# Moving VectorE's scaling of a finished pair between the two one-hots of the next, and dropping every second pace count on GpSimd

## The reference

```
for _ in range(3):
    x = segment_sum(vals[:, None] * x[cols], rows, num_segments=18750)
    acc = acc + x
out = acc / 4
rating = users_emb[users] @ items_emb.T + bias_user[users] + bias_item.T
return sigmoid(rating)
```

## Time and profile before

| what | us |
|---|---|
| median of 3 runs (lowest, highest) | 5386.34 (5384.41, 5394.33) |
| the profiled execution's own time | 5386.6 |
| its span, from first to last instruction | 5384.8 |
| VectorE busy | 4793.2 (89%) |
| TensorE busy (matmul) | 3361.2 (62%) |
| ScalarE busy | 2443.1 (45%) |
| GpSimd busy | 2415.1 (45%) |
| first halves, first to last scatter | about 1454 to 2288, 2715 to 3546, 3973 to 4807 |

### The profile page before, as it was taken

How to read it: one execution, slowest core, us unless ns; L and a number is a source line. 1 busy time by engine, 2 the same in 40 slices (tenths; PEclk the granted TensorE clock), 3 DMA queues, 4 the chain that set the end, 5 groups by cost and what they waited for, 6 DMA issues and landing times.

```text
span 5384.8 us, 195868 instructions
## 1 busy us (share of the span) xinstructions
PE 3361.2 (62%) x71235; PEld 2864.2 (53%) x71473; DVE 4793.2 (89%) x7569; ACT 2443.1 (45%) x4368; POOL 2415.1 (45%) x2161
## 2 busy tenths in 40 slices
PE   5600021111288888777678888867768888867767
PEld 4500011110277777666567777756657777766652
DVE  9989999999999999877799999967789999977778
ACT  0035555553366666500156666620046666640027
POOL 0038763330177777700067777730037777760000
PEclk9955555555699999999999999989989999989989
DMA  9960000300188778799968878889968777879999
GB/s 329 415 260 0 0 0 3 5 0 0 64 248 253 248 246 247 234 321 328 279 213 251 248 256 249 249 276 328 328 191 255 249 245 246 249 241 328 328 281 357
DMA packets 840272, 1191.20 MB, mean 221 GB/s; under 512 B 150792, under 2 KB 667583, under 8 KB 839825
## 3 DMA queue, kind: packets, MB, share of 16 engines
q1 hardware_dynamic: 716032, 816.66, 53.2%
q0 software_dynamic: 123872, 372.78, 18.0%
q10 hardware_dynamic: 304, 1.00, 0.1%
HBM read 638.35 MB, written 551.90 MB: 221 GB/s over the span
## 4 chain that ended last, share of the span: by engine, by line
DVE 28%; DMA 28%; issue 20%; POOL 9%; PE 6%; ACT 5%; SPq 1%; DVEq 1%; POOLq 0%; another core or an unknown queue 0%; ACTq 0%
DMA ring<-posts 15%; DMA posts<-ring 9%; POOL posts L775 9%; DVE store L1064 6%; PE psum L1501 4%; DVE total L861 3%; ACT new L695 3%; DVE store L1042 3%; DVE ring L1271 3%; DVE store L1043 2%; DMA out<-new 2%; DVE new L1243 2%; DVE ring L1256 2%; DVE ring L1295 2%; DMA ring<-lanes_d 1%
## 5 line engine op out<-in xcount | busy, mean ns | idle before, releaser
L775 POOL DMA_INDIRECT posts<-ring x1884 | 1852.6, 983 | 1740.6 <-DVE ring L1256 1154.0
L1477 PE MATMUL psum<-store,ring 128*128 x45216 | 2086.2, 197 | 497.9 <-DVE ring L1271 461.6
L1477 PEld LDWEIGHTS psum<-store,ring 128*128 128x128 bf16 x45216 | 1815.1, 100 | 769.2 <-issue 591.4
L695 ACT ACTIVATE new<-new 128x512 bf16<-128x512 uint8 x1884 | 1067.8, 614 | 0.0
L1271 DVE TENSOR_SCALAR ring<-ring,lane_f 128x1024 bf16<-128x1024 bf16 x1884 | 959.7, 551 | 23.4 <-DMA ring<-lanes_d 22.0
L1295 DVE TENSOR_TENSOR ring<-ring,wide_lane 128x1024 bf16<-128x1024 bf16 x948 | 612.9, 688 | 300.1 <-ACT ring L705 300.1
L1256 DVE TENSOR_TENSOR ring<-new 128x1024 bf16<-128x1024 bf16 x942 | 652.2, 692 | 93.8 <-ACT new L695 63.3
L693 ACT ACTIVATE ring<-new 128x512 bf16<-128x512 bf16 x942 | 585.9, 622 | 310.3 <-DVE new L1243 308.2
L750 POOL TENSOR_TENSOR ring<-store 128x1024 f32<-128x1024 f32 x157 | 369.6, 2354 | 660.6 <-DVE store L982 306.3
L1243 DVE TENSOR_TENSOR new<-psum,vals_m 128x512 f32<-128x512 f32 x942 | 644.1, 684 | 6.1 <-PE psum L1477 4.0
L1501 PE MATMUL psum<-ring 128*128 128x64 bf16 x11520 | 387.4, 193 | 188.7 <-DVE ring L1295 180.9
(11 more groups left out here) (228 smaller groups left out, 2666.1 us busy)
## 6 DMA issues: line engine op xcount, KB each, us to landing
ring<-lanes_d SPq DMA_DIRECT2D x471, 512.0 KB
ring<-posts SPq DMA_DIRECT2D x240, 772.0 KB, 6.7
store<-posts SPq DMA_DIRECT2D x234, 772.0 KB, 6.7
posts<-store SPq DMA_DIRECT2D x2, 30880.0 KB, 166.7
posts<-store SPq DMA_DIRECT2D x2, 30108.0 KB, 128.5
out<-new SPq DMA_DIRECT2D x96, 500.0 KB, 8.4
posts<-ring POOLq DMA_INDIRECT x1884
store<-L_rec_bias_item SPq DMA_DIRECT2D x1, 3125.0 KB, 13.8
```

The source lines that it names most:

```text
L695: last = nc.scalar.activation(digits[s][:, k, :], scaled_byte[s][k], ACT.Copy, scale=scale)
L775: pool.indirect_dma_start(out=posts[:, :], out_offset=bass.IndirectOffsetOnAxis(ap=dring[:, h, c:c + 1], axis=0), in_=msg[:, n, :], in_off ...
L1477: last = pe.matmul(psum[:, d % 4, (n % 2 * BLOCK + b) * F:(n % 2 * BLOCK + b + 1) * F], of, xflat[:, bass.ds(at_d[c] * F + (k * XT + x * F ...
```

## The change

Two edits, both in the first halves. On VectorE, the scaling of pair d-2 goes from before the wait for the lanes to behind the first one-hot of pair d. The one-hots, the scaling and the low parts are themselves the same instructions. On GpSimd, the count of `s_pace` is made only where the wait for `s_msg` stands, so before the even scatters; the odd ones are issued without one.

```diff
                         if n % 2 == 0:
                             pool.wait_ge(s_msg, i * 8 + (layer * DUOS + n // 2 + 1))
-                        pool.sem_inc(s_pace, 1)
+                            pool.sem_inc(s_pace, 1)
                         pool.indirect_dma_start(
...
                         dve.wait_ge(s_sent, i * 8 + (layer * DUOS + d + 1))
-                        if not (first and d < 2):
-                            if first and d == 2:
-                                dve.wait_ge(s_taken, layer * SPLITS + 2)
-                            scale(i, (d + 6) % 8, d - 2)
                         if j % 2 == 0:
                             dve.wait_ge(s_idx[j // 2], i * 32 + (layer * HALF_LOADS[j // 2] + h + 1) * 16)
                         for k in range(2):
                             last = nc.vector.tensor_scalar(hot[d % 2][:, k, :], idx[j // 2][:, j % 2 * 2 * CHUNK:(j % 2 + 1) * 2 * CHUNK],
                                                            lane_f[:, k:k + 1], None, ALU.is_equal)
+                            if k == 0 and not (first and d < 2):
+                                if first and d == 2:
+                                    dve.wait_ge(s_taken, layer * SPLITS + 2)
+                                scale(i, (d + 6) % 8, d - 2)
                         last.then_inc(s_hots, 1)
```

## The result

The changed kernel took 5403.4 us (median of 8 runs, 5395.45 to 5406.17) against 5389.12 us for the kernel before in the same runs (8, 5384.41 to 5399.11). The ratio is 1.0021, with a 95% interval of 1.0011 to 1.0031: slower by about 11 us, and clear of no change by the interval. (The medians lie 14.3 us apart, the means of the eight 11.7; the text goes by the ratio.) The forecast was 12.5 us on 5386.6, 5399.

The account below looks back on a forecast made before the run. GpSimd's scatter pace was taken as the bound; count 0, in step 0, lane waits 12.5 and out of step 0, on 5386.6, gave 5399 us; own range 5390 to 5421, whole range 5374 to 5421.

Parts of the forecast that it names:

- GpSimd is the bound: First halves: GpSimd's scatters, 1.265 us apart, set the pace; 628 make 794 us of a first half's 832.
- The count costs nothing: GpSimd's count before odd scatters: hidden under the scatter before, taken as 0 between bounds 0 and -14 us.
- In step, nothing changes: VectorE in step with GpSimd: pair stays 2.53 us, second one-hot still held from 0.50 to 0.70; 0 us.
- The wait for the lanes is what costs: VectorE's first one-hot needs its load 0.60 us earlier; late loads cost 12.5 us, ends 3 and 87.
- The first 0.20 costs nothing: Late lane loads: a wait's first 0.20 us is free, since the second one-hot would be held anyway.
- The 0.37 us for one late load: Scatters after the late load at 2247: three stretched by 0.37 us together; 0.25 us taken for each.
- Out of step, no difference: Scatters stretched when the step is lost: taken as 0, bounds all of the 43 us gone or as much again.
- ScalarE's cover: ScalarE gets scaled rows 0.40 us later, hidden by 178 us of waiting for scatters; 94 us if gone.
- Rival A: Lane loads land before 5.63 us or the hold swallows late ones: no change, 5388 us; chance 0.33.
- Rival B: One-hots apart halve the scatters' 43 us of stretching: faster, 5360 us, GpSimd's mean below 972 ns; chance 0.13.
- Rival C: VectorE becomes the bound, first one-hot also held: pair 2.73 us against 2.53, 188 us, 5575; chance 0.04.
- rival D: GpSimd's dropped count does nothing or is worth 14 us, 5385 with the forecast's 12.5; no separate chance given.

Follow-up runs that it names:

- e2: Kernel before with only GpSimd's count ahead of the odd scatters dropped; ratio to before 0.9998 (0.9989 to 1.0007).
- e4: Scaling put behind both one-hots, which stand together, in place of ahead of them; ratio to the kernel before 1.0296 (1.0282 to 1.0310).
- e3: Old instruction order, only the wait for the lanes put ahead of the scaling; ratio to the kernel before 1.0021 (1.0012 to 1.0030).
- e9: Changed order and count with the four lane buffers of e8, third chip; ratio to the kernel before 1.0003 (0.9994 to 1.0012).
- e8: Kernel before with four lane buffers, each layer's first body still on two, third chip; ratio to before 0.9998 (0.9989 to 1.0007).
- e5: Changed kernel with four lane buffers in place of two, second chip; ratio to the kernel before 1.0037 (1.0024 to 1.0051).
- e6: Kernel before with four lane buffers in place of two, second chip; ratio to before 1.0021 (1.0011 to 1.0030).
- a1: The changed kernel run once more, on the third chip; ratio to the kernel before 1.0005 (0.9996 to 1.0014).
- b1: The kernel before, unchanged, run once more on the third chip; 5364.61 us.

## Why the prediction was right, point by point

**GpSimd is the bound.** Right. The first halves lengthened by what the scatters did, 9 ns x 1884 = 17 of 19.5 us, while VectorE, at 89% of the span, was busy for 5 us less in all (4793.2 to 4788.2).

**The count costs nothing.** Right: gap 0.30, and 0.9998 in e2. Of the bounds, 0 and -14, it is the first.

**In step, nothing changes.** Right to the hundredth: 2.53, the first one-hot at 0.76 unheld, the second at 0.49 held and 0.70 long. With it falls the reading of the Trainium skill's SBUF page (section "Who interferes with whom") by which a one-hot would wait for the whole of a scatter: here the trace does not agree, since the one-hot took 0.48 from 0.76 into a scatter of 0.96. That VectorE and GpSimd hold each other at certain points is seen again in the 1.43 of e4.

**The wait for the lanes is what costs.** Right, and shown by e3, where it alone brings 1.0021. The term was 12.5 us; the ratio gives 11. Its parts were less good than its product, and three readings behind them were off.

- The 24 waits of the earlier trace rows are not 24 late loads: three are the starts of layers, with 13.1 of the 22.0 us. That leaves 21. How many loads would come late was guessed well all the same: between 5.63 and 6.23 us from issue landed 97 of the 268 loads that can be followed in the kernel before, 36%, where one in three was taken. Not all of them made a one-hot wait for 0.15 us or more; 102 did.
- "The first 0.20 costs nothing" was wrong. It looked at the second one-hot, which is held anyway, and not at the first, which a late load pushes over the next scatter's start: 0.18 of waiting cost 0.11 at 2033. The trace has 80 waits beyond 0.20 where 17 were before, 63 more, where 50 were taken.
- The 0.37 us for one late load was read in a stretch that was out of step already: in the earlier trace rows the scatter at 2245.88, ahead of the late one-hot, took 1.35. The 0.25 taken from it turned out near: the scatters grew by 16.8 us, 0.27 for each of the 63, or 0.21 for each of the 81 late loads more; single ones cost 0.11 (2033) and 0.44 (2013).

That the product comes out within 2 us of the ratio is thus partly luck. And the term isn't a constant of the kernel, as the prediction had it: it goes with how soon the loads land, and on the third chip it was about 3 us (0.0005) by the times and 9 by the scatters of one profile each.

**Out of step, no difference.** Taken as 0 between bounds of -43 and +43. e9 over e8 is 0.0005, with an interval of each of about 0.0009, e5 over e6 0.0016. It is not large; whether it is 0 or some 3 us is not settled, and why one execution of e5 had scatters of 1035 ns stays open. e3, with the old order and the whole cost, leaves little room for more.

**ScalarE's cover.** Right: it waited 512.0 us for landed scatters against 616.9 before, and was not missed.

Rival A (no change, the loads land before 5.63) is near to what happens on the third chip, where the time can't be told from no change, though 36 loads were late in place of 3; in the first comparison it failed, by 105 waits to 24. Rival B (faster, scatters less stretched) failed: 992 ns where it needed 972. Rival C (VectorE the bound) failed, since the pair stayed at 2.53. Of rival D the half that failed is the 14 us: the count was worth nothing.

## What to carry to other kernels

Moving an instruction to another place moves the waits in front of it too: ask of each wait that is moved ahead how much slack its transfer had, and compare that with the distance of the move (here 6.23 us from issue to use became 5.63, with transfers that take up to 7). Two engines that hold each other can settle into a step in which one gives way at a fixed point and the engine that is the bound runs free; a hold seen there is not waste, and an edit that changes no instruction, only their order, can still break the step (e4, 3%). An effect that hangs on a transfer's time should be measured on more than one chip: here it was 0.0021 (0.0011 to 0.0031) on one and 0.0005 (-0.0004 to 0.0014) on another. And before a price is read at one event, look whether the stretch was undisturbed ahead of it, and follow it until it is undisturbed again.

## What the runs showed of the hardware

- In the profiles of before, the change, e3, e4, a1 and b1, a one-hot of 128x1024 bf16 that starts 0.46 to 0.69 us into an unstretched scatter ends 1.18 to 1.19 into it: the one at 0.50 takes 0.70 us in place of 0.48, one at 0.65 takes 0.54. One that starts at 0.10, or from 0.70 to 0.78, takes 0.48, and the scatter keeps its 0.96.
- A product or one-hot that started more than about 0.1 us before the scatter and ends more than about 0.13 into it stretches the scatter, by about as much as it ends beyond 0.13: 1.07 at 2033.62, 1.35 at 2245.88, 1.43 at 2020.34 in e4, where a one-hot followed the product at once. The longest in e4 took 1.57. One that started only just before does not: the one-hot at 2014.01 took 0.52, and the scatter at 2014.07 stayed at 0.96.
- The scaling, which reads PSUM and SBUF, kept its time (678 to 694 ns in all 942 of e3) and did not stretch the scatter it lay over: from 2005.22 to 2005.90 it ran over the scatter's start at 2005.72, and that scatter took 0.96.
- A semaphore count between two indirect DMAs of GpSimd was free: 0.30 between them with it and without.
- The same 512 KB loads, in the same two programs, landed after 4.54 and 4.58 us (medians, b1 and a1) on the third chip and after 5.49 and 5.35 in the first profiles: 14.2 against 22.0 us of waiting with the kernel before, 25.1 against 61.6 with the changed one.
- In e4 TensorE's granted clock in the first halves was lower, 0.87 and 0.86 against 0.96 and 0.96 of full speed in the first two before, though it did the same products. Windows of e4, columns as in the earlier trace rows:

```profile
1454.00:2340.00 886.00, 696.68 (x14924) 633.20 (x14924) 733.60 (x1563) 532.42 (x1094) 672.65 (x626) 0.87 0.73 231
2770.00:3660.00 890.00, 697.98 (x14900) 633.69 (x14900) 735.88 (x1562) 531.83 (x1094) 675.43 (x629) 0.86 0.73 230
```

  Its busy time hardly moved (697 and 698 us against 687 and 683), and GpSimd was the bound in both, so nothing of the 160 us is put down to it.
